# Loading the GRU's input-side images: through a scratch in HBM, or straight from SBUF to SBUF

## What is computed

```python
def cell(h, x):
    gi = x @ W_ih + b_ih
    gh = h @ W_hh + b_hh
    i_r, i_z, i_n = jnp.split(gi, 3, axis=-1)
    h_r, h_z, h_n = jnp.split(gh, 3, axis=-1)
    r = jax.nn.sigmoid(i_r + h_r)
    z = jax.nn.sigmoid(i_z + h_z)
    n = jnp.tanh(i_n + r * h_n)
    h_new = (1.0 - z) * n + z * h
    return (h_new, h_new)
_, hs = jax.lax.scan(cell, initial_state, xs)     # x is (4, 512, 512) by then
out = x + hs
```

## Time and profile before

| | us |
|---|---|
| median of 3 runs | 2147.14 |
| lowest and highest | 2144.82, 2153.47 |
| the profiled execution, its device time | 2152.64 |
| its span, first to last instruction | 2150.9 |
| attention, until the first recurrent matmul (L648) | 546.3 |
| recurrence, first to last transpose `rzT` | 547.8 to 2139.5 |
| granted clock of TensorE, mean | 0.999 |

### The profile page before, as it was taken

How to read it: one execution, slowest core, us unless ns; L and a number is a source line. 1 busy time by engine, 2 the same in 40 slices (tenths; PEclk the granted TensorE clock), 3 DMA queues, 4 the chain that set the end, 5 groups by cost and what they waited for, 6 DMA issues and landing times.

```text
span 2150.9 us, 130641 instructions
## 1 busy us (share of the span) xinstructions
PE 2117.3 (98%) x58001; PEld 1692.1 (79%) x58001; DVE 1311.8 (61%) x5001; ACT 1130.8 (53%) x5055; POOL 188.2 (9%) x227
## 2 busy tenths in 40 slices
PE   8999999999999999999999999999999999999997
PEld 5665666667888888888888888888888888888776
DVE  4766667665556565666666565666566666666555
ACT  5775766665444444445454444454444444444444
POOL 4433333331000000000000000000000000000000
PEclk9999999999999999999999999999999999999999
DMA  6000000004201000001000000000000100000000
GB/s 224 1 21 2 2 21 2 1 1 139 97 21 27 26 20 24 21 22 28 22 25 20 26 22 28 18 25 21 23 23 24 26 22 24 19 26 22 20 9 9
DMA packets 78912, 62.04 MB, mean 29 GB/s; under 512 B 41840, under 2 KB 74124, under 8 KB 78348
## 3 DMA queue, kind: packets, MB, share of 16 engines
q1 hardware_dynamic: 77332, 50.40, 7.9%
q0 software_dynamic: 528, 3.15, 0.4%
q10 hardware_dynamic: 488, 0.15, 0.0%
HBM read 29.80 MB, written 16.78 MB: 22 GB/s over the span
## 4 chain that ended last, share of the span: by engine, by line
PE 95%; DVE 2%; issue 1%; ACT 1%; POOL 1%; DMA 0%; SPq 0%; POOLq 0%; DVEq 0%; ACTq 0%
PE ps L648 64%; PE ps L389 7%; PE ps L545 7%; PE ps L481 7%; PE ps L566 3%; PE ps L582 3%; PE ps L451 2%; PE ps L465 1%; DVE nT L1021 1%; PE ps L456 1%; DVE xb L1032 1%; ACT xb L818 1%; DVE ps L1026 1%; DMA x1T<-in_L_cond_W_emb 0%; POOL qk_rs L362 0%
## 5 line engine op out<-in xcount | busy, mean ns | idle before, releaser
L648 PE MATMUL ps<-wqkv,xb 128*4 128x128 f32 x49152 | 1495.8, 273 | 14.4 <-DVE xb L1032 10.3
L648 PEld LDWEIGHTS ps<-wqkv,xb 128*4 128x4 f32 x49152 | 1231.7, 87 | 247.6 <-DVE xb L1032 200.3
L1021 DVE STREAM_TRANSPOSE rzT<-ps 128x128 f32<-128x128 f32 x512 | 163.1, 318 | 333.1 <-PE ps L648 333.1
L823 ACT ACTIVATE r_pair<-rzT 128x8 f32<-128x8 f32 x512 | 107.8, 210 | 451.8 <-DVE rzT L1021 451.8
L1032 DVE TENSOR_TENSOR_SCAN xb<-z_trip,xb 128x24 f32<-128x24 f32 x1024 | 213.0, 208 | 188.1 <-ACT xb L818 129.8
L818 ACT ACTIVATE xb<-ps 128x16 f32<-128x16 f32 x1024 | 189.8, 185 | 163.5 <-DVE ps L1026 152.7
L481 PE MATMUL ps<-wih,x1T 128*32 128x192 f32 x3392 | 229.4, 326 | 0.1
L780 ACT ACTIVATE probs<-ps,negmax 128x512 f32<-128x512 f32 x256 | 173.2, 689 | 102.6 <-DVE negmax L953 102.5
L830 ACT ACTIVATE z_trip<-znT 128x8 f32<-128x8 f32 x512 | 109.3, 213 | 193.1 <-DVE znT L1021 192.7
L545 PE MATMUL ps<-wqkv,xnT 128*128 128x384 f32 x512 | 204.4, 487 | 1.0 <-ACT xnT L726 1.0
L798 ACT ACTIVATE ps<-seeds 128x256 f32<-128x256 f32 x512 | 194.3, 379 | 0.0
(11 more groups left out here) (87 smaller groups left out, 1375.2 us busy)
## 6 DMA issues: line engine op xcount, KB each, us to landing
gi_spill<-gi_image SPq DMA_DIRECT2D x64, 192.0 KB, 2.2
seeds<-gi_spill SPq DMA_DIRECT2D x226, 32.0 KB
seeds<-gi_spill SPq DMA_DIRECT2D x282, 16.0 KB
seeds<-blank SPq DMA_DIRECT2D x10, 384.0 KB, 3.4
out<-xb SPq DMA_DIRECT2D x240, 16.0 KB
xb<-in_x SPq DMA_DIRECT2D x3, 1024.0 KB, 5.6
wih<-in_L_cond_W_ih SPq DMA_DIRECT2D x1, 3072.0 KB, 16.8
seeds<-blank SPq DMA_DIRECT2D x1, 3072.0 KB, 20.5
```

Of the source, the lines that this page charges most:

```text
L648: last = nc.tensor.matmul(ps[QD * j:QD * j + B, bank, 0:P], hist_flat[:, first:first + 3 * B - 2:3], weights, start=False, stop=False, ski ...
L1021: return nc.vector.transpose(into[:].rearrange("p (r k b s) -> p k r s b", r=4, k=blocks, b=B, s=2), ps[:, bank, first:first + QD * blocks])
```

## The change

Every transfer of `fetch` reads the image in SBUF itself and serves one batch instead of four. The image gets a second buffer (block n uses half n % 2), and the spills, their semaphore and the scratch go. The eight rows of a wave lie on eight partitions of the image and go to eight slots of one partition of the ring. For lack of room the blank row moves into an unused end of `xb`. The order of SyncE's queue changes: each (wave, j) is split into two pairs of batches, due one step after the other, so a block has 32 due steps instead of 16 (block n of 2 and up: steps 32n - 17 to 32n + 14; block 1: steps 21 to 52). Waves 2 and 3 of block 0 keep their steps with two groups of two batches in each. Before step 0, SyncE issues waves 0 and 1 of each batch as soon as its image is there, and ScalarE's queue issues nothing. VectorE's evacuation of batch 0 of block n now waits for the landing of the fetches of block n - 2.

```diff
-        gi_image = sb("gi_image", [P, B, GCOL])
-        blank = sb("blank", [P, GCOL])
+        gi_image = sb("gi_image", [P, 2, B, GCOL])
...
+        blank = xb_flat[:, D + HIST * ENTRY:D + HIST * ENTRY + GCOL]
...
-        gi_spill = nc.dram_tensor("gi_spill", (2, B, P, GCOL), F32, kind="Internal").ap()
...
-        fetch_steps = {BLK * n - (FETCH_LEAD if n > 1 else 11) + due: (n, due) for n in range(1, N_BLK) for due in range(16)}
+        fetch_steps = {step: [] for step in range(T)}
+        for n in range(1, N_BLK):
+            for due in range(32):
+                fetch_steps[BLK * n - (FETCH_LEAD if n > 1 else 11) + due].append((n, due))
+        for due in range(16, 32):
+            fetch_steps[(6 if due < 24 else 12) + due % 8 // 2].append((0, due))
...
-        def fetch(queue, n, wave, j):
-            for first, done, count in seed_parts(n, wave):
-                rows = slice(QD * j + done, QD * j + done + count)
-                queue.dma_start(seeds[QD * j:QD * j + B, first:first + count, 0:2 * P],
-                                gi_spill[n % 2, :, rows, 0:2 * P]).then_inc(ld_gi[wave], 16)
-                queue.dma_start(seeds[QD * j + B:QD * j + 2 * B, first:first + count, 2 * P:3 * P],
-                                gi_spill[n % 2, :, rows, 2 * P:3 * P]).then_inc(ld_gi[wave], 16)
+        def fetch(queue, n, wave, j, batches):
+            for b in batches:
+                for first, done, count in seed_parts(n, wave):
+                    rows = slice(QD * j + done, QD * j + done + count)
+                    queue.dma_start(seeds[QD * j + b:QD * j + b + 1, first:first + count, 0:2 * P],
+                                    gi_image[rows, n % 2, b, 0:2 * P]).then_inc(ld_gi[wave], 16)
+                    queue.dma_start(seeds[QD * j + B + b:QD * j + B + b + 1, first:first + count, 2 * P:3 * P],
+                                    gi_image[rows, n % 2, b, 2 * P:3 * P]).then_inc(ld_gi[wave], 16)
...
+            sp.wait_ge(ld_blank, 16)
             for b in range(B):
-                spill(0, b)
-            sp.wait_ge(st_gi, 16 * B)
-            sp.wait_ge(ld_blank, 16)
-            for j in (0, 1):
-                fetch(sp, 0, 0, j)
-            for j in range(4):
-                fetch(sp, 0, 1, j)
-            spill(1, 0)
+                sp.wait_ge(s["gi_evac"], b + 1)
+                for wave in (0, 1):
+                    for j in range(4):
+                        fetch(sp, 0, wave, j, (b,))
...
-                if step in fetch_steps:
-                    n, due = fetch_steps[step]
-                    wave, j = divmod(due, 4)
-                    if due == 0:
-                        sp.wait_ge(st_gi, 16 * B * (n + 1))
+                for n, due in fetch_steps[step]:
+                    wave, part = divmod(due, 8)
+                    j, pair = divmod(part, 2)
+                    sp.wait_ge(s["gi_evac"], B * (n + 1))
                     sp.wait_ge(s["seeded"], step + 2)
-                    fetch(sp, n, wave, j)
-                if step - 1 in evac_steps:
-                    spill(*evac_steps[step - 1])
+                    fetch(sp, n, wave, j, (2 * pair, 2 * pair + 1))
...
-            act.wait_ge(st_gi, 16 * B)
-            act.wait_ge(ld_blank, 16)
-            for j in (2, 3):
-                fetch(act, 0, 0, j)
...
-                if n > 0 and b == 0:
-                    dve.wait_ge(st_gi, 16 * B * n)
-                nc.vector.tensor_tensor(gi_image[:, b, :], ps[:, bank, 0:GCOL], b_in[:],
+                if n > 1 and b == 0:
+                    for wave in range(4):
+                        dve.wait_ge(ld_gi[wave], gi_landed(n - 2, wave))
+                nc.vector.tensor_tensor(gi_image[:, n % 2, b, :], ps[:, bank, 0:GCOL], b_in[:],
                                         ALU.add).then_inc(s["gi_evac"], 1)
```

More of the change, by code:

```diff
@@ L172, in attention_gru_kernel @@
         TURN_STEPS, SEND_STEP, LAST_BLOCK = (3, 5), 7, N_BLK - 1
-        (ld_cond, ld_emb0, ld_emb1, ld_emb2, ld_emb3, ld_wqkv_first, ld_wqkv_rest, ld_x_first, ld_blank, ld_blank_mid, ld_blank_rest, ld_wout, ld_wih, ld_whh, ld_bias, ld_gi0, ld_gi1, ld_gi2, ld_gi3, ld_x, ld_g, st_gi, st_out) = (
+        (ld_cond, ld_emb0, ld_emb1, ld_emb2, ld_emb3, ld_wqkv_first, ld_wqkv_rest, ld_x_first, ld_blank, ld_blank_mid, ld_blank_rest, ld_wout, ld_wih, ld_whh, ld_bias, ld_gi0, ld_gi1, ld_gi2, ld_gi3, ld_x, ld_g, st_out) = (
             sem(n) for n in ("ld_cond", "ld_emb0", "ld_emb1", "ld_emb2", "ld_emb3", "ld_wqkv_first", "ld_wqkv_rest", "ld_x_first", "ld_blank", "ld_blank_mid", "ld_blank_rest", "ld_wout", "ld_wih", "ld_whh", "ld_bias", "ld_gi0", "ld_gi1", "ld_gi2", "ld_gi3",
-                             "ld_x", "ld_g", "st_gi", "st_out"))
+                             "ld_x", "ld_g", "st_out"))
         s = {n: sem(n) for n in (
@@ L217, in gi_landed @@
         def gi_landed(block_no, wave):
-            return 16 * sum(2 * 4 * len(seed_parts(n, wave)) for n in range(block_no + 1))
+            return 16 * sum(2 * 4 * B * len(seed_parts(n, wave)) for n in range(block_no + 1))
         def elements(step, half):
@@ L268, in _ @@
                     load_biases()
[L271 to L276, removed]
             def send_rows(m, b, i):
@@ L283, in fill @@
             def fill(first, end, landed):
-                sp.dma_start(seeds[:, first:end, :], blank[:].unsqueeze(1).broadcast_to([P, end - first, GCOL])).then_inc(landed, 16)
+                sp.dma_start(seeds[:, first:end, :], blank.unsqueeze(1).broadcast_to([P, end - first, GCOL])).then_inc(landed, 16)
             sp.wait_ge(s["blank_ready"], 1)
@@ L306, in _ @@
                     fill(first, first + 2, ld_blank_mid if step <= 4 else ld_blank_rest)
[L307 to L314, removed]
-                if step in fetch_steps:
-                    n, due = fetch_steps[step]
-                    wave, j = divmod(due, 4)
-                    if due == 0:
-                        sp.wait_ge(st_gi, 16 * B * (n + 1))
+                if step == 6:
+                    sp.wait_ge(ld_blank_mid, 16 * 4)
+                if step == 12:
+                    sp.wait_ge(ld_blank_rest, 16 * 6)
+                for n, due in fetch_steps[step]:
+                    wave, part = divmod(due, 8)
+                    j, pair = divmod(part, 2)
+                    sp.wait_ge(s["gi_evac"], B * (n + 1))
                     sp.wait_ge(s["seeded"], step + 2)
-                    fetch(sp, n, wave, j)
-                if step - 1 in evac_steps:
-                    spill(*evac_steps[step - 1])
+                    fetch(sp, n, wave, j, (2 * pair, 2 * pair + 1))
                 if m > 0 and SEND_STEP <= u < SEND_STEP + 2 * B:
```

## The result

| | before | after |
|---|---|---|
| median of the runs, us | 2146.74 | 2339.75 |
| lowest and highest | 2144.82, 2153.47 | 2338.9, 2349.71 |
| span of the profiled execution | 2150.9 | 2347.9 |
| granted clock of TensorE, mean | 0.999 | 0.967 |

The ratio is 1.090, 95% interval 1.0875 to 1.0932. The forecast was 2149 us, a time that cannot be told from before. It was wrong, and so was the range.

The account below looks back on a forecast made before the run. TensorE, busy 98% of the span, was taken to bound the kernel, with transfers hidden. Terms of 0, +0.4 (VectorE's wait) and +1.5 (instruction supply) made about +2 us: 2149 us as a median, range 2140 to 2160.

Parts of the forecast that it names:

- the pitch: SyncE's queue in the recurrence: 0.346 us an issue, so four fetches and two sends take 2.6 us of a 3.1 us step.
- SyncE's queue falls behind: Rival: at 0.60 us an issue, ScalarE and VectorE wait in the early blocks; +23 us, 2170 us; chance 0.07.
- Before step 0: Fetches before the recurrence: wave 0 lands by 534.1, covered by the last quarter projections and opening of the banks; gain nothing.
- The new wait of VectorE: Evacuation of block 3's batch 0 at step 52 waits for block 1's last fetches; +0.4 us, ends 0 and +3.
- TensorE's instruction supply: TensorE's issue stalls, 17.7 us before, may change with DMA traffic; +1.5 us taken, ends -13.8 and +13.8.
- the middle stretch: 98 us of the recurrence before, four spills and 40 fetches, without issue stalls; used to put the instruction term near nothing.
- The range: Whole kernel: 2140 to 2160 us, from the wait's ends, half the instruction term's ends and the spread of three runs.
- The transfers that cost their landing time: Rival: transfers of one queue do not overlap, so a block's 144 take 317 us instead of 99; +3200 us; chance 0.01.

Follow-up runs that it names:

- the control with 2256 cheap fetches: Kernel before, every fetch cut into four by columns, still from HBM into four partitions; 2157.2 us beside 2152.3 of before, ratio 1.0018.
- the kernel of transfers alone: New kernel computing no layers: SyncE issues each transfer form singly, then back to back; the change's fetch form took 635 ns median per issue.

## Why the prediction was wrong

**The step that failed is the pitch.** The prediction said "Four issues take 1.27 us, or 1.4 us at the pitch of 0.346", and "It fits". The pitch came from a row of the operation that was being removed: HBM to four partitions. The new transfer differed in both ends, and its issue measured 0.62 to 0.63 us, 0.684 from start to start and 0.70 with the pauses. The prediction did have an SBUF-to-SBUF row before it, the fill at 0.60 us, and read from it only that a fetch behind it is slower. Taken as the nearest row to the new form, which by its two ends it is, it would have given, with 0.04 us from an issue's end to the next, 142 x 0.64 + 16 x 0.64 = 101 us of queue a block against 99: a queue that is full, where the prediction has one with time to spare.

**The rival was right, its size was not.** "SyncE's queue falls behind", decided at 0.38 us an issue, is what happened, at the two places named, and had a chance of 0.07. It was priced at +23 us. Its places measured as follows: step 30 gave ScalarE a wait of 13.0 us (8 foretold), step 52 gave VectorE one of 23.3 (15 foretold). What was not priced are the other blocks. The rival counted bunched steps and took it that the queue recovers between them; at its pitch of 0.60 us that was true (158 x 0.60 = 95 us), at 0.684 the queue loses 9 us in every block, and with the pauses 12. Nor was the clock priced, 1.7 us for the step behind step 30 and some 24 us in all.

**Before step 0** the gain was put at nothing, with wave 0 landed by 534.1. The queue had already fallen behind there. Its 64 issues, 0.71 us each on the mean, run from 506.9 to 552.6. Those of batches 0 to 2 were to be out while the attention ran; batch 3's image was there at 529.1, and its first issue came at 541.7. So the first seed waited for the ring and began at 548.37 instead of 543.70. The cover named was the right one, and too short.

**The new wait of VectorE** was found in advance, with its place. It was priced at 0.4 us (0 to 3) and cost 23.3 there and 108.0 in 11 places. The other ten are not at places where the schedule is tight, but where the lag of the queue had grown by itself.

**TensorE's instruction supply**, +1.5 us: the stalls went from 17.7 to 29.5 us in the changed kernel, +11.8, near the far end that the prediction gave (+13.8). In the control with 2256 cheap fetches they were 21.1, and the total effect of everything was a ratio of 1.0018 (0 to 7 us). So the number of transfers does not make them grow by much; what does is open. The row it leaned on, the middle stretch, had 16 sends beside its 44 transfers, so 60 without a stall.

**The range.** By its own working (2149 + 2.6 + 7 + 6.3) its upper end is 2165 and not 2160. That decided nothing.

**The transfers that cost their landing time** (0.01) did not come. The Trainium skill (SBUF — State Buffer, The DMA setup-cost knee) speaks against many small transfers, and this change did lose. Its reason, though, a floor of about 2 us a transfer, is one of latency, and the kernel of transfers alone agrees with the figure. The timeline of SyncE's queue there shows the first four of the change's form, each issued when the one before had landed:

```profile
186.06 6.42 SPq L113 DMA_DIRECT2D ring<-held  x4
```

Three landings and a last issue make 6.42 us, so one is (6.42 - 0.64) / 3 = 1.9 us. What decided here was another price, that of the issue on its queue. For that the trace of before had medians of 0.24 to 0.60 us, by form. Of it the Trainium skill (DMA: Bandwidth & Descriptors, Anatomy of one DMA) gives, on POOL's path, about 50 ns for the sequencer's dispatch, beside a small and variable part for making the descriptors. POOL's issues of a fetch took 0.51 us here and the shortest issue of any queue 0.23, so the figure alone prices none of them.

## What to carry to other kernels

A queue that issues transfers is an engine with a busy time: multiply the number of issues by the time from one start to the next, and compare the sum with the period of the loop, not only in its tight places. Take the price from a row whose two ends are in the same memories, and spread over as many partitions, as those of the new transfer, and where there is none, bound it by the dearest issue in the trace. A removed stop in HBM is worth nothing where no engine waited for it.

## What the runs showed of the hardware

- The issue of a transfer on SyncE's queue took, in the median, 0.24 to 0.31 us from HBM into 2, 4 or 8 partitions, 0.42 into 32 and 0.58 to 0.62 into one; 0.57 to 0.68 from SBUF to SBUF in seven forms; and 0.30 from 8 partitions of SBUF to HBM. Twice the rows cost no more (0.60 for 16 rows), and half the rows hardly less (0.57 for 4).
- The same fetch issued by POOL took 0.51 us, less than from SyncE.
- After TensorE had stood for 12 us behind the wait at step 30 its granted clock was at 0.50, and the next 96 matmuls took 4.56 us instead of 2.8 to 2.9.
